# One-hot matrices of slots written in pairs of tiles, and read by TensorE with a step of two

## What is computed

```python
h = einsum('btd,od->bto', x, W) + delta(x, A[adapter], Bm[adapter], scalings)
xt = h.reshape(4096, 512)
shared_out = einsum('ted,edh->th', gelu(einsum('th,ehd->ted', xt, Wsh_up)), Wsh_down)     # 2 experts, D = 256
probs = softmax(xt @ W_router)                                                           # 16 experts
top_v, top_i = top_k(probs, 2)
gate = sum(one_hot(top_i) * top_v[..., None], axis=1)
routed_out = einsum('ted,edh->th', gelu(einsum('th,ehd->ted', xt, Wrt_up)) * gate, Wrt_down)
out = x + shared_out + routed_out
```

## Time and profile before

| | |
|---|---|
| median of 3 runs | 628.64 us (628.38 to 630.75) |
| profiled execution, its time | 626.79 us |
| profiled execution, span from first to last instruction | 625.1 us |
| PE busy | 603.3 us, 97% |
| DVE busy | 429.2 us, 69% |
| ACT busy | 325.5 us, 52% |
| POOL busy | 173.1 us, 28% |
| granted TensorE clock | 1.000 |

### The profile page before, as it was taken

One profiled execution on the slowest core, in us unless ns is written; L12 is line 12 of the kernel. 1 busy time (PEld: TensorE's weight loads), 2 busy tenths in 40 slices (PEclk: granted clock), 3 DMA queues, 4 the chain that ended last, 5 costly groups with the idle time before them and its releaser, 6 DMA issues.

```text
span 625.1 us, 13266 instructions
## 1 busy us (share of the span) xinstructions
PE 603.3 (97%) x4075; PEld 406.4 (65%) x4077; DVE 429.2 (69%) x798; ACT 325.5 (52%) x503; POOL 173.1 (28%) x254
## 2 busy tenths in 40 slices
PE   7999999999989979799999999999999999999996
PEld 5555555555556656577777777777777777767672
DVE  3768999999979984455555555555555563689896
ACT  1347587686965413355555555555555554333331
POOL 1000001101000002233333333333333305777750
PEclk9999999999999999999999999999999999999999
DMA  8899983433361524855555556555555438999977
GB/s 290 358 374 422 422 288 134 165 138 135 135 206 63 169 86 152 297 163 164 166 166 155 154 163 168 161 156 159 162 168 158 155 120 299 345 313 388 396 292 273
DMA packets 50293, 135.62 MB, mean 217 GB/s; under 512 B 6432, under 2 KB 6432, under 8 KB 47968
## 3 DMA queue, kind: packets, MB, share of 16 engines
q1 hardware_dynamic: 38544, 97.83, 42.1%
q0 software_dynamic: 11440, 37.50, 21.5%
q10 hardware_dynamic: 288, 0.03, 0.0%
HBM read 86.31 MB, written 49.02 MB: 217 GB/s over the span
## 4 chain that ended last, share of the span: by engine, by line
PE 65%; DVE 25%; DMA 6%; ACT 2%; issue 2%; SPq 1%; POOL 0%; ACTq 0%; POOLq 0%; DVEq 0%
PE bank L1497 16%; PE bank L1478 16%; PE bank L1417 10%; PE bank L1404 10%; PE bank L1462 5%; DVE rtw L935 5%; DMA act_in<-xT 4%; PE bank L1487 3%; PE bank L1314 2%; DVE lot_max L910 2%; DVE x_max L947 2%; DVE c_chunk L903 2%; DMA region<-xc_dram,slot_idx 1%; DVE tmp L964 1%; DVE arena L964 1%
## 5 line engine op out<-in xcount | busy, mean ns | idle before, releaser
L1189 DVE SCALAR_TENSOR_TENSOR region<-bank,scale,region 128x512 f16<-128x512 f32 x79 | 59.3, 751 | 118.5 <-ACT region L813 118.5
L1478 PE MATMUL bank<-rtw,region 128*128 x948 | 116.5, 273 | 0.0
L1497 PE MATMUL bank<-rtw,tmp 128*128 x474 | 115.3, 380 | 0.3 <-DVE tmp L1197 0.3
L1478 PEld LDWEIGHTS bank<-rtw,region 128*128 128x128 f16 x948 | 92.7, 98 | 10.1
L575 POOL DMA_INDIRECT region<-xc_dram,slot_idx x79 | 77.8, 985 | 61.3 <-POOL slot_idx L572 61.3
L1404 PE MATMUL bank<-act_in,shw 128*128 128x256 f16 x768 | 87.8, 273 | 0.4 <-ACT tmp L769 0.4
L1417 PE MATMUL bank<-shw,hid 128*128 128x512 f16 x384 | 86.2, 379 | 1.7 <-DVE rtw L1256 1.5
L820 ACT ACTIVATE region<-bank,un_dn 128x512 f32<-128x512 f32 x79 | 54.3, 687 | 55.4 <-PE bank L1497 55.4
L1404 PEld LDWEIGHTS bank<-act_in,shw 128*128 128x128 f16 x768 | 74.5, 98 | 12.8 <-issue 0.9
L595 POOL DMA_INDIRECT rtw<-r_dram,pos x64 | 66.0, 1031 | 42.7 <-issue 37.2
L1497 PEld LDWEIGHTS bank<-rtw,tmp 128*128 128x128 f16 x474 | 46.3, 98 | 39.1 <-issue 1.4
(11 more groups left out here) (164 smaller groups left out, 796.2 us busy)
## 6 DMA issues: line engine op xcount, KB each, us to landing
r_dram<-region SPq DMA_DIRECT2D x79, 256.0 KB, 3.2
rtw<-rt_w SPq DMA_DIRECT2D x16, 1024.0 KB, 11.7
act_in<-xT SPq DMA_DIRECT2D x16, 512.0 KB, 5.0
xc_dram<-rows SPq DMA_DIRECT2D x16, 512.0 KB, 4.3
xcT_dram<-hid SPq DMA_DIRECT2D x16, 512.0 KB, 2.9
rtw<-x_rows SPq DMA_DIRECT2D x15, 512.0 KB, 5.3
rtw<-xcT_dram SPq DMA_DIRECT2D x10, 512.0 KB, 5.6
out<-rtw SPq DMA_DIRECT2D x9, 512.0 KB, 5.5
```

Source lines behind the costliest of these rows:

```text
L1189: nc.vector.scalar_tensor_tensor(xgT[s][:, 1], R_XT[s][:].rearrange("p (k t) -> p k t", k=HK), col(scale, C_ALL).bitcast(F32), xgT[s][:, 0 ...
L1478: last = mm(R_UP[s][:, 0:D], xgT[s][:, xp, k, :], rtw[:, bass.ds(e, 1), w0:w0 + D].rearrange("p a d -> p (a d)"), start=(k == 0 and n == 0 ...
L1497: last = mm(R_DN[s][:], midT[s][:, xp, m, :], rtw[:, bass.ds(e, 1), w0:w0 + H].rearrange("p a h -> p (a h)"), start=(m == 0 and n == 0), s ...
```

## The change

`in_part` is laid out as (pair of tiles, place, tile of the pair) in place of (tile, place), as `in_val` is. For that GpSimd writes `iota_p` with each number twice (256 elements, in place of 128), VectorE's L1154 compares it with pairs of `lo_f`, and TensorE reads each standing matrix with a step of two elements. The elements per instruction, the number of instructions, their order on each engine and all waits stay as they are; only the iota's size differs.

```diff
-        inv_bufs = carve([((GRP, P), F16), ((GRP // 2, NJ_ALL, 2), F16)] * 2 + [((NJ_ALL, 2), F16)])
+        inv_bufs = carve([((GRP // 2, P, 2), F16), ((GRP // 2, NJ_ALL, 2), F16)] * 2 + [((NJ_ALL, 2), F16)])
...
-        iota_p = xam[1][:, 0:P // 2].bitcast(F16)
+        iota_p = xam[1][:, 0:P].bitcast(F16).rearrange("p (l b) -> p l b", b=2)
...
-            nc.gpsimd.iota(iota_p, [[1, P]], base=0, channel_multiplier=0,
+            nc.gpsimd.iota(iota_p, [[1, P], [0, 2]], base=0, channel_multiplier=0,
                            allow_small_or_imprecise_dtypes=True).then_inc(sort_iotas, 1)
...
-                def by_tile(v):
-                    return v.rearrange("p (a b) -> p a b", b=2).unsqueeze(2).to_broadcast([P, GRP // 2, NJ_ALL, 2])
+                def by_tile(v, n=NJ_ALL):
+                    return v.rearrange("p (a b) -> p a b", b=2).unsqueeze(2).to_broadcast([P, GRP // 2, n, 2])
...
-                nc.vector.tensor_tensor(in_part[s], iota_p.unsqueeze(1).to_broadcast([P, GRP, P]),
-                                        lo_f[:, s, at].unsqueeze(2).to_broadcast([P, GRP, P]), ALU.is_equal)
+                nc.vector.tensor_tensor(in_part[s], iota_p.unsqueeze(1).to_broadcast([P, GRP // 2, P, 2]),
+                                        by_tile(lo_f[:, s, at], P), ALU.is_equal)
...
-                    last = mm(INV[:, 0:NJ_ALL], in_part[g % 2][:, n, :], in_val[g % 2][:, n // 2, :, n % 2],
+                    last = mm(INV[:, 0:NJ_ALL], in_part[g % 2][:, n // 2, :, n % 2], in_val[g % 2][:, n // 2, :, n % 2],
                               start=(g == 0 and n == 0), stop=(g == NG - 1 and n == GRP - 1))
```

## The result

The changed kernel takes 625.33 us (median of 7 runs, 623.45 to 626.05), the kernel before 629.88 (7 runs on the same chip, 627.09 to 630.83). The ratio is 0.9935, with a 95% interval of 0.9914 to 0.9956: 2.8 to 5.4 us faster. The forecast was a gain of 4.2 and a time of 624.4; the time is 0.9 above that, and the kernel before, too, came out 1.2 above the median of its first three runs.

What follows compares the result with a forecast made beforehand. TensorE bounds the kernel, but in the inversion it waits for VectorE's L1157. Eight L1154 at 0.534 us less give 4.27, minus a 0.05 stall: 628.64 - 4.2 = 624.4 us, range 623.5 to 626.9 (8 in 10).

Steps and rivals of the forecast that it cites:

- VectorE's new duration: L1154 in the inversion: 682 ns in place of 1216, 0.534 us less each, 4.27 us for the eight.
- The stepped loads, x = 0: TensorE's L1390 loads with a step of two: x, the loss per group of eight, taken as 0, at most 0.42 us.
- The upper bound of 92 ns: Slowest pace for a stepped L1390 load-and-matmul pair, from L1347's 32-bit loads; x = 0.42 us, time 626.8 us.
- Rival 2: Inversion: stepped loads take twice as long, 78 ns a pair; gain 2.7 us, time 625.9; chance 0.20.
- No stall at places(4): VectorE's places(4), writing over the third group's buffer, starts at 217.33 as TensorE finishes at 217.30; stall 0 to 0.05 us.
- What is late next: End of the inversion: VectorE still ends last, TensorE waits some 0.9 us at the last group; gain at L1417 4.2 us.
- The x for add_x(2): Input of add_x(2) in the inversion: there at 217.5, wanted at 219.0, 1.5 us to spare.
- The iota: GpSimd's iota of 256 elements: 0.24 or 1.01 us, ending near 190, needed at 208.4; no cost on the path.
- 4.2 us carried to the end: Behind 232 us everything moves as a whole, so the inversion's 4.2 us passes through; span 625.1 to 620.9.
- (b): Trace stretch from the routed loop's first up product to its last down product, measured afterwards; 262.4 us before, 264.2 changed.
- The 1.85 us between the profiled run and the median: Whole kernel: the runs' median, 628.64, lies 1.85 us above the profiled 626.79; kept in the forecast of 624.4.
- Rival 3: Gather landing at 256.43 us: queued behind one more 512 KB load, it gives the gain back; 627 to 628; chance 0.06.

Runs made afterwards that it cites:

- Experiment 1: Changed kernel with its layout and TensorE's step of two kept, but VectorE writing one place-run at a time, without neighbouring pairs; ratio to before 1.0135, interval 0.9991 to 1.028.
- experiment 2: Kernel before with lo_f written twice, pairs being neighbouring places of one tile, standing matrices contiguous; 656.54 us against 657.98 for the changed kernel, ratio to before 0.9993.
- experiment 3: Changed kernel plus 32 load-and-matmul pairs of 16 columns at each step of 1, 2, 4, 8 behind the last inversion group; 25.0, 25.0, 33.4, 62 ns a pair.
- Experiment 4: Changed kernel with the change kept for the odd groups only, even ones written and read as before; 624.65 us, ratio to before 0.9935.
- the spread kernels: Before and changed kernels with SP's four L451 loads put behind routed-loop stores; changed one 621.25 us, ratio 0.9879 (0.9887 on another chip); before one 0.992.
- before again: The kernel before, repeated without any edit; ratio to its other runs 1.0154, interval 1.003 to 1.0277.
- step only: Changed kernel with layout and TensorE's step of two, but VectorE writing runs of places without pairs; ratio to before 1.0135, median 662.94 us.
- experiment 5: Kernel before and changed kernel repeated without edit; ratio 1.0154 for before, 0.9894 and 0.9937 for the changed kernel's second and third repeats.
- half of the groups: Changed kernel with the change in the odd groups only; 624.65 us against 625.57 for the changed kernel on the same chip, ratio to before 0.9935.

## Why the prediction came out right

- *VectorE's new duration.* Forecast 682 ns from L1152's form, measured 684. Experiment 1 takes the pairs away and the gain goes with them; experiment 2 gets them another way, and the gain is there.
- *The stepped loads, x = 0.* Right: 97 ns each, a group 0.29 to 0.33 us ahead of what follows, 25.0 ns a pair at either step. The upper bound of 92 ns from 32-bit elements was far from it: the same span of bytes did not mean the same cost. Rival 2, with a chance of 0.20 the largest beside the forecast, is refuted by experiment 3.
- *No stall at places(4).* I had the third group done at 217.30 and places(4) from 217.33. Shifted by the 1.22 us of this execution, the third group starts at 216.84, to the hundredth as worked out, and VectorE's L1152 of places(4) at 217.34. They just meet, without a stall and with about 0.04 us to spare (the third group is through at 217.30 on that count), closer than such a sum can be trusted to tell.
- *What is late next.* I forecast 0.9 us left at the last group, counted by starts; by starts it is 0.86 (227.23 + 0.31 to 228.40), and 0.71 by the profile, which counts from the modelled end. VectorE still ends last. Experiment 4 shows the gain in proportion to the groups, as it must be while that holds. The x for add_x(2) was there in time: VectorE has no pause.
- *The iota.* It took 1.51 us, more than both bounds (0.24 and 1.01), which were rows of another size. It ended at 191.4, 18 us ahead of its reader, so this cost nothing.
- *4.2 us carried to the end.* As a sum it holds: 4.25 us at L1417, 4.1 by the ratio, 4.55 between the medians. As a chain it is looser than I wrote. I took what lies behind 232 us for fixed, and (b) isn't: leaving out the spread kernels it varies from 261.6 to 265.3 with the length of the gather's wait (2.5 to 3.3 us) and with whether the clock falls behind it (some 1.8 us). The rows fit 259 + wait + 1.8 for a fall within 0.3 us, with two exceptions, before again and step only, 1.1 and 1.2 above, where the clock stayed low longer (6.8 us, against 3.4 in the others). The forecast of the profiled span, 620.9, missed by 2.7 us for this: 1.2 from stage 1 and 1.8 from the loop, less 0.3 from the last stage.
- *The 1.85 us between the profiled run and the median.* I added them without asking what they were. They are as much as a fall of the clock costs, and the clocks in experiment 5 make that the likely reason, though the clocks of those first runs are not on record. That both kernels have the fall in most of their runs is what let 4.2 us pass to the end; half of the groups, at a clock of 1.000 in three of four runs, shows that a shift of 2 us can remove it. In that respect it was luck that the total came out right.
- *Rival 3* named that place, but not the right mechanism: the wait did not grow by another load, the clock fell behind it. The kernel before has the same fall, at least as often by the clocks of the last chip, so it doesn't tell against the change.

## What to carry to other kernels

Where a 16-bit two-input VectorE instruction repeats one element along its innermost run, look for a layout whose innermost run is two neighbouring elements in every operand; the side that reads the result may then be able to step over the pairs, and it is worth measuring that load by itself before paying for a second layout. A gain on an engine counts in full only until the engine that waits for it has no wait left: work out both walks, and say by how much the next one is behind. A profile is one execution: before a sum starts from it, compare its clock and time with the other runs. And look at the longest single wait of the engine that bounds the kernel: here four loads that nobody needed for 250 us started on one signal, and spreading them gave about as much as the change under study (4.3 us between the medians).

## What the runs showed of the hardware

- A stepped load of 128 x 128 16-bit elements, with a matmul of 16 columns: 25.0, 25.0, 33.4 and 62 ns a pair at steps of 1, 2, 4 and 8, in one execution.
- A VectorE comparison of 1024 16-bit elements: 1216 ns where one input repeats one element along its innermost run, 684 ns where that run is two neighbouring elements in both inputs.
- A VectorE write with a step of two at one element per tick lasts 1300 ns where the contiguous one lasts 1216, for 1024 elements; by starts, 1.19 and 1.13 us.
- TensorE's clock fell to the lower level behind waits for the gather of 2.7, 3.1, 3.2 and 3.3 us, and did not behind waits of 2.5 and, once, 3.1. In the step-only kernel a wait of 2.49 us at the sixth group was followed by 24 matmuls in 4.01 us, not 2.78, and in experiment 3 the gather's wait of 2.37 us by a clock of 0.50 from 268 us. So the length of the wait alone, at this size, doesn't settle it; what else does is open.
- It also fell without a wait just ahead: in experiment 3, after 4.7 us of loads with 16-column matmuls, with TensorE busy throughout; the last wait, of 0.70 us, had ended 5 us earlier. The stretches there:

```profile
232.00:233.00 1.00, 1.00 (x19) 1.00 (x19) 0.00 (x0) 0.00 (x0) 0.00 (x0) 1.00 0.00 0
233.00:234.00 1.00, 1.00 (x13) 0.75 (x13) 0.24 (x1) 0.00 (x0) 0.00 (x0) 0.80 0.00 0
234.00:236.00 2.00, 2.00 (x6) 0.63 (x5) 0.00 (x0) 0.00 (x0) 1.04 (x2) 0.50 0.39 132
```

- On two chips ScalarE stood still in the last stage for 10.4 to 12.5 us at the longest, in every kernel, with a releaser that the profile calls remote and no instruction of this core. On the chip with the last stage of 109 us its longest wait there was 4.2 us. Why is open; no run tried it.
